# A 6 KB DMA per head moves from SP's queue to ACT's in a dual attention kernel

## The reference, cut to what matters

```
xn  = layernorm(x)
A   = causal attention of xn: 16 heads of 8 channels, rotary positions, then an output projection
B   = a graph of 6 nodes; node c: q, k, v = scaled linear maps of earlier nodes,
      o = attention(q Wq, k Wk, v Wv) Wo with 8 heads of 16 channels and no mask,
      node[c] = act_w[c] * o + q
out = x + A + layernorm(node[5])
```

## Time and profile before

| | us |
|---|---|
| median of 3 executions | 1687.93 |
| lowest, highest | 1687.03, 1692.68 |
| the profiled execution, its own time | 1698.56 |
| its span, first to last instruction | 1696.7 |
| mean granted clock of TensorE in it | 0.950 |
| one pass of the BL loop (a step 4 to the next), by the trace | about 112 |

### The profile page before, as it was taken

How to read it: one execution, slowest core, us unless ns; L and a number is a source line. 1 busy time by engine, 2 the same in 40 slices (tenths; PEclk the granted TensorE clock), 3 DMA queues, 4 the chain that set the end, 5 groups by cost and what they waited for, 6 DMA issues and landing times.

```text
span 1696.7 us, 65726 instructions
## 1 busy us (share of the span) xinstructions
PE 1558.3 (92%) x25626; PEld 799.3 (47%) x25626; DVE 1187.0 (70%) x1207; ACT 1117.3 (66%) x2219; POOL 446.1 (26%) x930
## 2 busy tenths in 40 slices
PE   6999999999999899898998998989989989899995
PEld 4467676644434444344443443444434434444442
DVE  7767666687857677578676775676866857767582
ACT  3366566677857677567676775676766857676582
POOL 4321113306042151240511513315115033150110
PEclk9899999999999999999999999999999999999997
DMA  7121112233222231232222312323123222231112
GB/s 225 38 94 44 42 43 80 96 105 127 71 91 83 67 117 51 64 126 68 95 72 66 124 55 72 108 66 113 55 65 127 66 88 78 74 121 49 53 34 58
DMA packets 116109, 138.86 MB, mean 82 GB/s; under 512 B 14945, under 2 KB 90466, under 8 KB 115682
## 3 DMA queue, kind: packets, MB, share of 16 engines
q1 hardware_dynamic: 115810, 134.54, 24.9%
HBM read 65.04 MB, written 62.39 MB: 75 GB/s over the span
## 4 chain that ended last, share of the span: by engine, by line
PE 73%; DMA 12%; SPq 6%; issue 4%; DVE 2%; ACT 2%; POOL 1%; ACTq 0%; DVEq 0%; POOLq 0%
PE s L942 44%; PE cps L1033 21%; PE misc L937 9%; DMA qs<-mrows 4%; DMA dram_rec_b<-sums 3%; DMA dram_raw_b<-csb 3%; SPq L407 2%; SPq L439 2%; ACT probs L723 2%; DMA ks<-dram_qk_b 1%; SPq L480 1%; SPq L454 1%; DMA ctx_b<-dram_raw_b 0%; DMA ks<-dram_qk_a 0%; SPq L433 0%
## 5 line engine op out<-in xcount | busy, mean ns | idle before, releaser
L899 DVE TENSOR_REDUCE neg_max<-s 128x1 f32<-128x1024 f32 (+7 forms) x1024 | 1123.2, 1106 | 465.9 <-PE s L942 408.0
L723 ACT ACTIVATE probs<-s 128x512 f32<-128x512 f32 x1792 | 974.5, 598 | 438.9 <-PE s L942 432.2
L942 PE MATMUL s<-qs,ks 99*32 99x512 bf16 (+1 forms) x7680 | 689.5, 384 | 93.1 <-DMA qs<-mrows 59.6
L942 PE MATMUL s<-ks,qs 96*32 96x512 bf16 (+2 forms) x7680 | 623.3, 380 | 8.7 <-DMA ks<-dram_qk_a 4.3
L1033 PE MATMUL cps<-probs,vs 128*32 128x256 f32 (+1 forms) x7296 | 616.0, 385 | 0.3 <-ACT probs L723 0.3
L942 PEld LDWEIGHTS s<-qs,ks 99*32 99x32 bf16 x7680 | 220.2, 95 | 473.7 <-ACT probs L723 249.2
L1033 PEld LDWEIGHTS cps<-probs,vs 128*32 128x32 f32 x7296 | 250.2, 112 | 185.0 <-issue 17.7
L942 PEld LDWEIGHTS s<-ks,qs 96*32 96x32 bf16 x7680 | 225.9, 98 | 97.2 <-issue 25.2
L579 POOL TENSOR_TENSOR mparts<-neg_max,zeros 128x8 bf16<-128x8 f32 x128 | 25.7, 201 | 935.2 <-DVE neg_max L899 934.8
L942 PE MATMUL s<-mask_k,ident_h 128*32 128x128 bf16 x1024 | 101.2, 221 | 0.0
L942 PE MATMUL s<-mask_q,ident_h 128*32 128x128 bf16 x1024 | 78.6, 224 | 0.6 <-issue 0.6
(11 more groups left out here) (122 smaller groups left out, 620.2 us busy)
## 6 DMA issues: line engine op xcount, KB each, us to landing
dram_qk_b<-parts SPq DMA_DIRECT2D x48, 384.0 KB, 3.5
qs<-dram_qk_b SPq DMA_DIRECT2D x96, 192.0 KB
ks<-dram_qk_b SPq DMA_DIRECT2D x96, 192.0 KB
dram_qk_b<-parts SPq DMA_DIRECT2D x48, 256.0 KB, 3.3
dram_raw_b<-csb SPq DMA_DIRECT2D x96, 128.0 KB, 4.1
dram_qk_b<-parts SPq DMA_DIRECT2D x48, 128.0 KB, 3.4
vsrc<-srcT SPq DMA_DIRECT2D x12, 512.0 KB, 4.6
ctx_b<-dram_raw_b SPq DMA_DIRECT2D x48, 128.0 KB
```

What stands on the lines that cost most here:

```text
L723: nc.scalar.activation(buf[:, lo:hi], s2[bank][:, 0:hi - lo], ACT.Exp, scale=scale).then_inc(exp_done, 1)
L899: last = ve.tensor_reduce(neg_max[k % 2][:, t:t + 1], s1[n % 2][:, lo:hi], AX.X, ALU.max, negate=True)
L942: last = te.matmul(dst[c0:c0 + STRIP, :], lhsT[:, c0:c0 + STRIP], rhs, start=start, stop=stop, tile_position=(0, c0))
```

## The change

SP no longer waits for the copy of the maxima and no longer issues the DMA. ACT issues the same DMA on its own queue behind the copy; before it, it waits on the semaphore that its own copy raises. The semaphore that PE and ACT wait for (`mrow_in`) and the bytes are the same. It concerns 128 DMAs, one for each unit.

```diff
@@ SP, phase() @@
                     if k == SPREAD_AT.get(kind):
                         spread_reciprocals(kind, r, b)
-                    if kind_at(kind, k, 1):
-
-                        sp.wait_ge(mrow_sb, u)
-                        sp.dma_start(qs[(k - 1) % RING][MROW:KALL, :].rearrange("a (i n) -> a i n", n=128),
-                                     mrows[(k - 1) % 2][:, :]).then_inc(mrow_in[(k - 1) % RING], 16)
                     if k in READ_AT.get(kind, {}):
                         read_before(kind, r, b, READ_AT[kind][k], "contexts")
@@ ACT, phase() @@
                             nc.scalar.copy(mrows[(k - 1) % 2][:, :], misc_rows).then_inc(mrow_sb, 1)
+                            act.wait_ge(mrow_sb, u)
+                            act.dma_start(qs[(k - 1) % RING][MROW:KALL, :].rearrange("a (i n) -> a i n", n=128),
+                                          mrows[(k - 1) % 2][:, :]).then_inc(mrow_in[(k - 1) % RING], 16)
                         which = kind_at(kind, k, 2)
```

## The result

The kernel after takes 1749.04 us, the median of 4 runs (1745.64 to 1751.36); the kernel before takes 1688.88, the median of 4 (1687.03 to 1692.68). The ratio is 1.0352, with a 95% interval of 1.0325 to 1.0378: 60 us slower. The profiled execution of after took 1745.64 us. It was the shortest of its four, and the profiled one of before the longest of its four, so the two spans (1743.8 and 1696.7) differ by only 47 us. What follows reads the traces for where time is, and the ratios for how much.

What follows compares the result with a forecast made beforehand. PE, busy 92%, was taken to bound the kernel, with nothing in hand against a late exponential. Cost 99 us less gain 17 us gave 82 us, added to the median 1687.9 for 1770 us; range 1705 to 1812.

Steps and rivals of the forecast that it cites:

- The wait for the maxima goes: PE's 17 waits for the maxima's DMA, 59.6 us, mostly BL step 3, were to vanish; PE busy below 90%.
- What is late next: BL step 4: node's matmuls wait over 3 us for POOL's product, low clock follows; gain 17 us including BE and B0.
- The hold of ACT by the issue: Each of 128 issues holds ACT's queue as it held SP's, 0.81 us; total cost 99 us.
- The wait for the own copy: ACT waits 0.03 us after its copy and needs about 0.10 us from issue to next instruction.
- No slack: Exponentials 0.98 us late make PE equally late; 70 BL steps at 0.84 to 1.02 us, 66 us.
- Pass A at 0.94 us a step: 16 steps of AL lose 0.94 us each, 15 us; A0 and AZ lose 4.5 us.
- Which delays the wait for POOL's product takes up: Step 3's delay in BL and BE falls into the wait for `rec_b` and costs nothing; otherwise 11 us.
- The lower clock, charged the same: Low clock expected again behind BL's node matmuls, charged the same 2.4 us; gain left at 1.1 us a pass.
- the eleven hidden steps: Ten steps 3 of BL and one of BE, charged nothing; 11 us if the `rec_b` wait did not exist.
- free issue: ACT's sequencer hands the DMA over, leaving only its own-copy wait, 13 us; 1684 us, or 1660 us; chance 0.11.
- short issue: Issue on ACT takes 0.36 us, as SP's writes to DRAM; 34 us slower, 1722 us; chance 0.08.
- late landing: Maxima's DMA still lands late in step 3, held up by SP's earlier transfers; 108 us slower, 1796 us; chance 0.08.

Runs made afterwards that it cites:

- sp_both: Kernel before, SP issuing the maxima's DMA before waiting for the reciprocals' landing and, in step 2, before the contexts' wait; 1678.96 us, ratio 0.9881.
- double: Kernel after plus a second identical DMA from ACT into a spare tile; 1838.07 us, ratio 1.0842 to the kernel before.
- own_wait: Kernel before with ACT waiting for its own copy of the maxima, SP still issuing the DMA; 1703.54 us, ratio 1.0057.
- act_free: Kernel after with the node's matmuls in turns 4 and 6 and POOL's product moved to step 4; 1697.69 us, ratio 0.9989 to before.
- sp_free: sp_both_node with POOL's product moved to step 4, behind that step's maxima parts; 1617.12 us, ratio 0.9529 to before.
- act_a: Kernel before with ACT issuing the maxima's DMA for pass A's 32 heads only, SP the other 96; 1706.64 us, ratio 1.0053.
- sp_both_node: sp_both with the node's matmuls in turns 4 and 6 of step 4 instead of 1 and 5; 1658.05 us, ratio 0.9771 to before.

## Why the prediction was right, and where it was off

The sign and the mechanism are as predicted; the kernel became 60 us slower where the sum had 82, and the time is 21 us below the forecast of 1770 and inside the range. Step by step:

- **The wait for the maxima goes.** Right: its line is gone, in BL, BE and B0. The share of PE was said to fall below 90% and just did not: 1576.7 of 1743.8 us is 90.4%.
- **What is late next.** Right: the node's matmuls stand 3.03 us in the pass shown ("over 3 us"; 2.2 to 3.6 over the ten), and the lower clock follows. By the prediction's own numbers PE would stand 472.35 - 467.9 = 4.45 us, and that is sp_both, without ACT's delays: 48.1 / 11 = 4.4. Gain 17 us predicted, 20 measured without ACT (sp_both); a pass of BL is 1.1 to 1.4 us shorter there by the traces and B0 1.9, as forecast, while the 1.8 us of BE do not show (1.4 us longer, in one execution of each).
- **The hold of ACT by the issue, about 0.81 us from SP's row.** Right in kind and 10% high: 0.73, one behind the other (double). The dispatch of some 50 ns in the Trainium skill ("DMA: Bandwidth & Descriptors", "Anatomy of one DMA — SWDGE (gpsimd) path"), which would have given 1689 us by the estimate in the prediction, stands there for a DMA issued from GpSimd, and no run here issues one from it. What an issue takes from ACT here is 729 ns.
- **The wait for the own copy, 0.03 + 0.10 us.** Too low: by these terms the wait alone makes the exponentials 0.17 us late (438.05 + 0.03 + 0.10 against 438.01), and own_wait shows 0.23. The two errors nearly cancel, which is luck: 0.98 us late by the prediction, 1.0 by the trace (1.23 - 0.21).
- **No slack: PE is late by as much.** Right for pass B. Steps 1, 2, 3, 5 and 6 of BL are 0.87 to 1.01 us longer in after than in sp_both, as charged (0.84 to 1.02). act_free has 7.0 us a pass more than sp_free, against 7.6 by the prediction's list with step 3 counted; that the two are so close is in part luck, as step 4's issue is free there and more of PE's work runs at half clock.
- **Pass A at 0.94 us a step.** Wrong. This term was mis-sized: 15 us for AL and some 5 for A0 and AZ, and 9 measured for both (act_a), 0.56 to 0.64 a step in AL. The slack is about 0.4 us there. I had taken a single row, the weight load 0.05 us behind an exponential, as proof that nothing is in hand. It showed that PE waits at that point, and not that ACT can't make it up: there was a pause of 0.67 us on ACT right behind that pair.
- **Which delays the wait for POOL's product takes up.** Counted too low. The prediction lets the delay of step 3 fall into that wait, at no cost, and charges step 2 in full. The pass shown, in after and then in sp_both:

```profile
477.59 0.37 ACT L727 COPY csb<-cps 128x256 f32<-128x256 f32 x1
488.19 0.26 ACT L706 COPY mrows<-misc 24x128 bf16<-24x128 bf16 x1
499.14 0.37 ACT L727 COPY csb<-cps 128x256 f32<-128x256 f32 x1
```

```profile
462.82 0.37 ACT L736 COPY csb<-cps 128x256 f32<-128x256 f32 x1
468.69 3.67 PE misc L944 x4
475.26 0.25 ACT L718 COPY mrows<-misc 24x128 bf16<-24x128 bf16 x1
485.32 0.37 ACT L736 COPY csb<-cps 128x256 f32<-128x256 f32 x1
```

From step 4's `csb` to the node's first matmul (481.92 in after) it is 4.33 us in place of 5.87; from there to the copy of the maxima 6.27 in place of 6.57; from that copy to the next `csb` 10.95 in place of 10.06. The means of the ten passes say the same: 1.67 us less in front of the node, 0.46 less behind it (PE is busy at 0.50 for 3.2 us there, and for 4.1 in sp_both), and 0.96 us more for step 4's own issue. So step 4's charge of 0.84 us was right, and the chain of waits of after has that issue on it (488.47). But the wait takes up 1.67 us of the delays ahead of it, all of step 3's 0.97 and 0.7 of step 2's: counted from step 2's `csb`, the node's matmuls start only 0.3 us later in after (27.75 in place of 27.48), although PE lost 1.95 us in steps 2 and 3.
- **The lower clock, charged the same.** The prediction leaves the stretches at 0.50 as they are wherever the change doesn't remove a wait. At the loop's edge PE is busy at 0.50 for 3.2 us a pass in after and for 4.6 in sp_both, and steps 7 and 0 together cost 1.1 us where the list has about 1.9. In act_free it goes the other way, and they cost 2.7.

The cost was 99 us in the prediction and 80 in the runs (after against sp_both). act_free against sp_free has 81, and there the list says 110, as the eleven hidden steps come out. The traces of after and sp_both, of one execution each and 63 us apart, place what is missing: pass A 11 us less than charged, BL 20 less, and B0, BE and T together 4 less. Of BL's 2 us a pass, 0.7 are the wait, some 0.5 the clock in step 4 and 0.8 the loop's edge. Why the stretches at the lower clock became shorter, with pauses as long as before (the earlier trace rows have 6.13 us at 0.50 behind a pause of 2.98 us, the table of after 3.73 us at 0.54 behind 3.29), was not tried, and stays open. A version with the DMA on GpSimd's queue was not tried either.

Of the rivals, free issue and short issue fall by the row of 729 ns, and late landing by the missing wait.

## What to carry to other kernels

An engine that is 66% busy has no room for 0.7 us if another waits for its every result: before you move an issue, look at how long behind the result its consumer starts, and at whether the engine has a pause a few instructions on in which to make it up. A queue that stands in a wait in any case (SP here, for its own write) can issue for nothing. And when a wait is taken away, ask at once what is late next, then again: with the issue kept on SP, the 59.6 us were worth 8 alone, 20 with the chain behind them earlier, and 80 once the node's matmuls and POOL's order had moved as well. A wait that stays also hides part of a new cost: the 60 us between before and after are a cost of 80 and a gain of 20, and neither can be read from them.

## What the runs showed of the hardware that was not expected

- The issue of the same DMA took less on ACT (729 ns median) than on SP (812), with a longest one of 1337 ns.
- A wait of ACT for the semaphore of its own copy costs 0.23 us, as it ends the overlap with the next instruction and the next one starts 0.18 us behind its end.
- A pause of PE of 3.03 us was followed by a granted clock of 0.50 (2.78 us of work), as one of 5.52 was before. Behind the pauses of sp_both_node in step 4 (none over 3.1 us) the lower clock followed in seven passes of ten.
